# A factor inversion moved behind a norm, and first lower parts moved ahead of others

## The reference

```
q, k, v = heads of x @ Wq.T, x @ Wk.T, x @ Wv.T      # 16 query heads, 4 key/value heads, 128 wide; q, k rotated (cos, sin)
qf, kf = elu(q) + 1, elu(k) + 1
state = running sum of kf v^T ; z = running sum of kf     # causal linear attention
o = (qf . state) / (qf . z + 1e-6)
x1 = layernorm(x + o @ Wo.T)
h = fwht(x1 * SU_ug) / 64
g = silu(h @ W_gate.T * s_gate) * (h @ W_up.T * s_up)
out = layernorm(x1 + (fwht(g * SU_dp) / 64) @ W_down.T * s_down)
```

## Time and profile before

| | us |
|---|---|
| median of 3 runs | 2294.93 (2291.66 to 2295.72) |
| profiled execution, own time | 2294.09 |
| its span | 2292.3 |
| PE busy | 2252.4 (98%) |
| DVE busy | 1830.6 (80%) |
| ACT busy | 1273.6 (56%) |
| POOL busy | 1126.9 (49%) |

### The profile page before, as it was taken

How to read it: one execution, slowest core, us unless ns; L and a number is a source line. 1 busy time by engine, 2 the same in 40 slices (tenths; PEclk the granted TensorE clock), 3 DMA queues, 4 the chain that set the end, 5 groups by cost and what they waited for, 6 DMA issues and landing times.

```text
span 2292.3 us, 32686 instructions
## 1 busy us (share of the span) xinstructions
PE 2252.4 (98%) x10226; PEld 1823.2 (80%) x10226; DVE 1830.6 (80%) x2482; ACT 1273.6 (56%) x2285; POOL 1126.9 (49%) x1004
## 2 busy tenths in 40 slices
PE   9899999999999999999999999999999999999998
PEld 7677878787878786788888778888888888888887
DVE  7877787868686868788888897787888788868877
ACT  7666666667676767243444555454445545554543
POOL 5666776767676767455544733322342133303311
PEclk9999999999999999999999999999999999999999
DMA  4021211102020115777678532223223322222313
GB/s 157 35 70 38 70 47 55 64 37 72 30 73 32 69 65 190 256 258 255 238 260 269 172 129 74 106 88 110 88 88 101 111 88 95 94 79 86 104 60 102
DMA packets 132710, 252.87 MB, mean 110 GB/s; under 512 B 44576, under 2 KB 45344, under 8 KB 122880
## 3 DMA queue, kind: packets, MB, share of 16 engines
q1 hardware_dynamic: 132608, 251.60, 32.7%
HBM read 188.11 MB, written 63.44 MB: 110 GB/s over the span
## 4 chain that ended last, share of the span: by engine, by line
PE 71%; issue 11%; POOL 9%; DVE 6%; ACT 2%; DMA 1%; SPq 0%; POOLq 0%; ACTq 0%; DVEq 0%
PE pj L626 16%; PE pj L709 11%; PE pnum L709 6%; PE pj L723 5%; PE psc L709 5%; PE pst L709 4%; PE psc L723 4%; PE pj L636 3%; PE pnum L723 3%; PE psc L657 3%; PE pnum L677 3%; PE pnum L680 3%; PE pst L723 2%; POOL fb L1416 1%; POOL fa L1415 1%
## 5 line engine op out<-in xcount | busy, mean ns | idle before, releaser
L1445 POOL TENSOR_TENSOR wcs<-wcr 128x256 f32<-128x256 f32 x64 | 67.6, 1056 | 514.4 <-DVE wcl L1187 505.4
L1482 POOL TENSOR_TENSOR tb<-tb,sinb 128x512 f32<-128x512 f32 x160 | 224.1, 1401 | 79.7 <-ACT tb L1007 79.4
L1485 POOL TENSOR_TENSOR Ql<-tb,Qh 128x512 fp32r<-128x512 f32 x128 | 171.2, 1340 | 65.6 <-ACT Qh L1016 65.6
L547 PE MATMUL pj<-woh,oh 128*128 128x512 f32 x512 | 202.1, 395 | 0.0
L626 PE MATMUL pj<-xah,wqh 128*128 128x512 f32 x500 | 198.2, 396 | 3.2 <-DVE Kf L1322 2.4
L547 PE MATMUL pj<-woh,ol 128*128 128x512 f32 x512 | 200.1, 391 | 0.0
L547 PE MATMUL pj<-wol,oh 128*128 128x512 f32 x512 | 199.8, 390 | 0.0
L626 PE MATMUL pj<-xah,wql 128*128 128x512 f32 x500 | 194.9, 390 | 0.0
L626 PE MATMUL pj<-xal,wqh 128*128 128x512 f32 x500 | 194.8, 390 | 0.0
L1310 DVE TENSOR_TENSOR pj<-pj,cosb 128x512 f32<-128x512 f32 x156 | 108.3, 695 | 69.9 <-ACT tb L1007 69.8
L1492 POOL TENSOR_SCALAR_AFFINE_SELECT Ah<-Ah 128x512 fp32r<-128x512 f32 x128 | 101.8, 795 | 112.7 <-DVE Al L1351 112.2
(11 more groups left out here) (287 smaller groups left out, 7115.3 us busy)
## 6 DMA issues: line engine op xcount, KB each, us to landing
num_scratch<-no SPq DMA_DIRECT2D x128, 256.0 KB, 2.4
nt<-num_scratch SPq DMA_DIRECT2D x32, 1024.0 KB, 5.4
rb<-rden_scratch SPq DMA_DIRECT2D x32, 1024.0 KB, 6.7
wdr<-wd_scratch SPq DMA_DIRECT2D x128, 256.0 KB, 3.2
wcr<-in_wg SPq DMA_DIRECT2D x64, 256.0 KB, 2.8
wcr<-in_wu SPq DMA_DIRECT2D x64, 256.0 KB, 3.1
xst<-in_xT SPq DMA_DIRECT2D x34, 256.0 KB, 3.8
xr<-in_x SPq DMA_DIRECT2D x32, 256.0 KB, 5.6
```

Of the source, the lines that this page charges most:

```text
L547: last = nc.tensor.matmul(py[s][:, :], a[s][:, h, :], b[:, h, :], start=(h == 0 and i == 0), stop=(h == H - 1 and i == 2))
L1482: nc.gpsimd.tensor_tensor(tb[c][:, :], tb[c][:, :], sinb[:, :], ALU.mult).then_inc(sin_done, 1)
L1485: nc.gpsimd.tensor_tensor(Ql[g % 2][:, c, :], (tb[c] if c else Kf)[:, :], f32(Qh[g % 2][:, c, :]), ALU.subtract).then_inc(lo_done, 1)
```

## The change

Three edits. The addition of 1e-6 and the reciprocal become two functions; the addition for `da` goes ahead of the division of step 1, and the reciprocal goes from the end of step 1 to step 2, between that step's norm and its division. In step 31 the three lower parts of the first weights go ahead of the norm of block 30. The lower parts of the first four columns all go into step 31, and the sums of the last block, 31, come after them; the scale factors (`sg`, `su2`) come after these, so ACT's wait for them moves from the head of the third stage to the first tanh.

```diff
                 if n:
                     act.wait_ge(h_lo, k if f else k - FB)
+                else:
+                    act.wait_ge(sc_step, 2)
...
             steps(act, step)
-            act.wait_ge(sc_step, 2)
...
-            def reciprocals(k, a):
+            def guarded(k, a):
                 dve.wait_ge(d_in, 16 * (k + 1))
                 nc.vector.tensor_scalar_add(a[:, :], a[:, :], 1e-6).then_inc(d_step, 1)
+
+            def inverted(k, a):
                 dve.wait_ge(d_step, 2 * k + 1)
                 nc.vector.reciprocal(a[:, :], a[:, :]).then_inc(d_step, 1)
...
+                if at == NC - 1:
+
+                    dve.wait_ge(f_lo, NM)
+                    for i in (0, 2, 1):
+                        weights_lo(0, i)
                 if at >= 1:
                     norm(1 - s, n - 1)
+                if at == 1:
+                    guarded(1, da)
+                if at == 2:
+                    inverted(1, da)
                 if at + 2 < NC:
                     divide(s, n + 2, m * 2 + j // 2 + 1)
...
-                if at == 1:
-                    reciprocals(1, da)
...
                 if at == NC - 1:
-
-                    dve.wait_ge(f_lo, NM)
-                    weights_lo(0, 0)
-                    columns_lo2(0, 0)
-                    columns_lo2(0, 1)
-                    weights_lo(0, 2)
-                    weights_lo(0, 1)
+                    for i in range(4):
+                        columns_lo2(0, i)
...
-                if n == 0:
-                    sums(1, NC - 1, NC // 2 - 1, NC - 1)
-                    columns_lo2(0, 2)
-                    columns_lo2(0, 3)
...
             steps(dve, step)
+            sums(1, NC - 1, NC // 2 - 1, NC - 1)
             dve.wait_ge(csc_in, 32)
```

More of the change, by code:

```diff
@@ L1132, in between @@
                 if (kind, g, c) == ("A", 1, 3):
-                    reciprocals(0, da0)
+                    guarded(0, da0)
+                    inverted(0, da0)
                 if (kind, g) == ("Q", 3):
```

## The result

The changed kernel is slower: 2301.88 us in the median of 7 runs, against 2293.32 for the kernel before on the same chip; the ratio is 1.0034, with a 95% interval of 1.0024 to 1.0044, so 5.5 to 10 us. The forecast was 2302.1. The profiled execution took 2301.94 us, its span 2300.2.

A forecast was written before the change was run, and what follows sets the result against it. PE is busy 98% of the span, so only its waits change the time. Second stage 7.2 plus seam 0.4 gives 7.6 us; on 2294.09 that is 2301.7, with half of 0.84 added 2302.1 us; range 2297.5 to 2305.5.

The forecast's parts named there:

- The chain behind the reciprocal: Second stage: reciprocal, store, factors' load and division of block 4 run in series; block 2's norm ends at 971.1.
- The stop at block 2: Second stage: PE stops ahead of block 2's transposes for DVE's late norm, 5.9 us, taken as 6.0.
- the 2.55 us stop: Second stage: PE's wait ahead of block 1's transposes for DVE's norm; claimed to stay, since POOL's sums set it.
- The clock: Second stage: PE runs at half clock after its stop at block 2, costing 1.2 us, bounds 1.2 to 1.6.
- The seam: Seam into the third stage: product 2 starts earlier, but PE waits at products 3 and 4; 0.4 us slower.
- the norm 1308.0, where it was 1306.1: Seam: block 30's norm on DVE ends at 1308.0 instead of 1306.1, behind the weight parts' turns with POOL.
- The sum: Whole kernel: second stage 7.2 plus seam 0.4, so 7.6 us slower; forecast 2302.1 us.
- Product 2's gain is kept: Rival, seam: weight parts don't hold POOL up; seam -1.9 or -4.2 us, total 2299.8 to 2297.5; 17%.
- The delay spreads: Rival, second stage: later blocks' loads meet in the queue, another 4 to 6 us, 2306 to 2308; 12%.
- Faster: the load is hidden: Rival, second stage: early norm lets the reciprocal end by 951.2, so PE sees no load; 2288 to 2290; 6%.
- The turns: DVE and POOL share a port lock held per instruction; at the seam the second weight part takes about 3.6 us.
- the second rival's: Prediction's seam remark: without the port lock, the sum would be this rival's instead of the forecast's.

The follow-up runs named there:

- e2_stage: The kernel before with only the change's edit of the inversion (addition and reciprocal moved), old seam: 2301.84 us, ratio 1.0036.
- e3_ahead_of_norm: e2_stage with the reciprocal one place earlier in step 2, between the lower part and the norm: 2296.1 us, ratio 1.0008.
- e4_root: e2_stage with POOL's inverse root of block 1 between its two pairs of sums in step 1, not behind both: 2299.89 us, ratio 1.0024.
- e5_filler: e2_stage with 23 unused matmuls ahead of block 2's transposes, where PE would stand still: 2300.33 us, ratio 1.0026.
- e10_early_root: The kernel before, with addition and reciprocal ahead of step 1's division and POOL's root of block 1 ahead of both pairs of sums: 2293.3 us, ratio 0.9992.
- e6_root30: The kernel before with POOL's root of block 30 between its two column sums, not behind them: 2293.91 us, ratio 0.9999.
- e7_seam_root30: The kernel before with the change's seam edits and POOL's root of block 30 between its two column sums: 2292.78 us, ratio 0.9992.
- e11_best: e10_early_root with the change's seam: 2290.51 us, ratio 0.9981 to the kernel before.
- e8_early: The kernel before, with addition and reciprocal ahead of step 1's division and POOL's root of block 1 between its sums: 2292.77 us, ratio 0.9990.

## Why the prediction was right

- *The chain behind the reciprocal.* Held to tenths: reciprocal at 953.63 (said 953.8), load issued 959.29 (959.4), division at 963.85 (964.0), norm of block 2 ended 970.94 (971.1). The division began 4.56 us after the load's issue, as the 4.6 of before had it. That this is so close is in part luck: the same load took 4.8 to 5.4 us to land in e2_stage, e3_ahead_of_norm, e4_root and e5_filler.
- *The stop at block 2.* 5.64 us (said 6.0). The step before, the 2.55 us stop stays (2.48).
- *The clock.* This term was mis-sized: said 1.2, at most 1.6, measured 14.09 - 11.37 = 2.7 us in this execution. The working took the slow stretch from the one behind a 3.02 us stop, 2.70 us long. Behind 5.64 us it was 5.6 us long, all at about half speed. In e2_stage and e4_root the same term was 1.6 and 1.4, the latter behind the longest stop of all (5.93 us), so the length of the stop alone doesn't set it. The second stage as a whole: 8.6 us by the table, said 7.2, within the bounds (7.1 to 9.9).
- *The seam.* Said 0.4 us slower, measured 0.4 faster by DVE's queue, 0.76 by the table, and 0.85 over four pairs. The mechanism was right: product 2's stop went, a stop ahead of product 4 came, and product 6 moved by tenths. So were three of its sizes (the middle weight part 3.43 us, said 3.6; the norm 2.58; POOL's sums stretched). The step that failed is "the norm 1308.0, where it was 1306.1": counted from `ve`, the norm ended 7.34 us later now (1308.70 to 1316.04) and 5.93 before, a delay of 1.4 us and not 1.9, as each turn was one to three tenths shorter than reckoned. Of the columns behind it the second and the fourth were to cost 0.5 us more than before, and the first four cost 0.1 more. ACT now waits 1.52 us for `ga`, and no stop of PE in these rows comes from that; `ga` itself stands 18.6 us behind `ve`, where it stood 19.1 behind it.
- *The sum.* The two errors, +1.4 and -0.8 to -1.2, nearly cancel, so the total came out closer than its two terms. That 2302.1 lies within 0.3 us of the measured median is luck as well: the kernel before came out at 2293.32 beside this run, 1.6 below the 2294.93 on which the forecast was built. What can be compared is the difference, 7.6 forecast and 7.8 (by the medians 8.6) measured.
- *The rivals.* "Product 2's gain is kept" fell in its mechanism: the weight parts do hold POOL up. Its number isn't far off: 0.4 to 1.3 us of 4.2 is kept, and the mean of 0.85 lies about midway between the forecast's 0.4 slower and this rival's least gain, 1.9. "The delay spreads" fell: from block 3 to block 29 the changed kernel takes 316.80 us, before 316.71. "Faster: the load is hidden" fell too, and e3_ahead_of_norm, which ended 1.0 us past its point, bears that point out for PE's timing of before. Its second half, an early norm, wasn't reached: in e4_root the norm ended 12.2 us behind block 0's transposes, where 8.1 was wanted, so what such a norm would bring with the reciprocal behind it stays open. What it wanted, a gain from the inversion's place, comes from the other direction: e10_early_root.
- *The turns.* The reading of the rows by instructions and not by shared bandwidth is borne out: the middle weight part (3.43 us for 1.21), the norm (2.58 for 0.55) and the second column part (ended 1.1 us behind POOL's sum) each run on past the end of POOL's sum by no more than their own length, while the reciprocal keeps its 3.35 us beside POOL in every profile. The Trainium skill (SBUF — State Buffer, section "SBUF: two separate sides") has the pair as an exclusive lock, held for a whole instruction; the rows of after agree (3.43 us for 1.21). Where the prediction says that without the lock the sum would be "the second rival's", it is the first of its list, the kept gain, that fits.

## What to carry to other kernels

An instruction whose result goes out to memory and comes back should be costed with its whole chain: here 3.35 us of DVE work carried 2.3 of store and 4.6 of load behind it, and moving it later by 10.5 us into idle time cost 8. When a wait is shortened, move both its ends in the reckoning: the waiting engine arrives earlier at its next wait. Where two engines take turns, as DVE and POOL do here, filling one's idle time can move the turn lost instead of removing it (0.85 us gained out of 3.3 filled); count the end of the queue that both serve, not the wait that goes.

## What the runs showed of the hardware

- The clock's loss isn't one size. Behind the stop of about 2.5 us at block 1 the granted clock stayed 1.00 in before, after and e3_ahead_of_norm, and fell in e2_stage, e5_filler, e6_root30 and e7_seam_root30, with 1.6 us lost (block 2 at 27.08 in e6_root30, 25.48 before, with the same second stage). The window of before behind the stop:

```profile
954.00:960.00 6.00, 6.00 (x29) 5.02 (x29) 5.08 (x7) 3.06 (x5) 1.35 (x1) 1.00 1.01 355
```

And of e6_root30:

```profile
954.00:960.00 6.00, 5.95 (x21) 4.86 (x22) 3.92 (x5) 3.05 (x5) 0.00 (x0) 0.72 1.00 336
```

It fell behind every stop of 4.47 us or more that had no filler (three profiles), and cost 1.4 to 2.7 us. What decides a single case is not settled here. A stop of this kind is priced at a range, and its removal can be worth more than its length, by up to 1.6 us at block 1. In e2_stage and e5_filler the loss behind block 1 fell into the wait for the load: that is why the stop at block 2 is 4.47 us in e2_stage and 5.64 in the changed kernel.
- A sum of POOL's took 5.58 us beside DVE's reciprocal and division (e11_best), though the reciprocal runs its 3.35 us and though two like sums ran 1.29 us each beside it before. The same sum took 5.58 us in e10_early_root, and one that began near the reciprocal's end took 4.21 in e8_early; each ended 1.2 us after the division had. Why the reciprocal held POOL up here and not there was not tested.
